# Routing rows of a mixture-of-experts kernel: first-choice rows leave once their indices exist, the row tags are rewritten in two parts, and GpSimd takes over two more output blocks and layer 1's early rows

## The reference, cut to what matters

```
x = L0_attn_x                                   # (32, 256, 128)
xn = layernorm(x)
x = x + attention_over_heads(xn) + experts0(xn) # layer 0
xn = layernorm(x)
x = x + long_convolution(xn) + experts1(xn)     # layer 1
return x

experts(x): logits = x @ W_gate                 # 8 experts
            top_w, top_i = top_k(logits, 2)     # weights by softmax
            out[t] = sum over the 2 choices of  w * (gelu(x[t] @ W_in[e] + b_in[e]) @ W_out[e] + b_out[e])
```

## Time and profile before

| what | value |
|---|---|
| runs, us | 1220.97, 1222.44, 1225.87 (median 1222.44) |
| profiled execution, span in us | 1227.7, with 19103 instructions |
| PE busy | 1013.8 us, 83% of the span |
| DVE busy | 747.2 us, 61% |
| POOL busy | 748.1 us, 61% |
| ACT busy | 584.5 us, 48% |
| chain that ended last, by engine | PE 37%, POOL 26%, DVE 14%, DMA 11%, issue 9%, ACT 3% |

### The profile page before, as it was taken

How to read it: one execution, slowest core, us unless ns; L and a number is a source line. 1 busy time by engine, 2 the same in 40 slices (tenths; PEclk the granted TensorE clock), 3 DMA queues, 4 the chain that set the end, 5 groups by cost and what they waited for, 6 DMA issues and landing times.

```text
span 1227.7 us, 19103 instructions
## 1 busy us (share of the span) xinstructions
PE 1013.8 (83%) x6498; PEld 856.5 (70%) x6498; DVE 747.2 (61%) x980; ACT 584.5 (48%) x1526; POOL 748.1 (61%) x655
## 2 busy tenths in 40 slices
PE   5646687789999999999435699999598999999994
PEld 4522333378888888888325699989588888888884
DVE  7877999999999999999989653111400200000018
ACT  1300110167777878778425872000066666666651
POOL 4147776558888888888674067677534544454430
PEclk9868887799999999999858699999899999999998
DMA  9913323326556565565271035999659676776749
GB/s 286 378 69 130 132 101 113 113 80 185 167 168 180 168 182 173 163 185 161 80 311 69 1 108 170 313 312 319 231 154 303 190 196 194 201 191 195 191 148 353
DMA packets 120245, 226.03 MB, mean 184 GB/s; under 512 B 16961, under 2 KB 80405, under 8 KB 118102
## 3 DMA queue, kind: packets, MB, share of 16 engines
q1 hardware_dynamic: 102164, 188.45, 50.5%
q0 software_dynamic: 17600, 35.71, 8.0%
q10 hardware_dynamic: 386, 0.66, 0.2%
HBM read 157.33 MB, written 67.42 MB: 183 GB/s over the span
## 4 chain that ended last, share of the span: by engine, by line
PE 37%; POOL 26%; DVE 14%; DMA 11%; issue 9%; ACT 3%; SPq 0%; POOLq 0%; DVEq 0%; ACTq 0%
POOL BG L319 12%; PE ps L819 9%; POOL y_tok L523 9%; PE ps L832 9%; PE ps L861 7%; DMA FF<-sorted_x 5%; POOL sorted_x L515 5%; DMA TPB<-in_kpad 3%; DVE BG L1168 3%; PE ps L927 2%; PE ps L806 2%; PE ps L774 1%; DVE stats L1023 1%; PE ps L937 1%; PE ps L963 1%
## 5 line engine op out<-in xcount | busy, mean ns | idle before, releaser
L523 POOL DMA_INDIRECT y_tok<-FF,yidx x284 | 277.8, 978 | 204.3 <-ACT FF L603 142.3
L515 POOL DMA_INDIRECT sorted_x<-XN,idx x256 | 246.5, 963 | 95.3 <-issue 85.6
L832 PEld LDWEIGHTS ps<-FF 128*128 128x128 f32 x2272 | 264.8, 192 | 19.6 <-issue 9.0
L832 PE MATMUL ps<-FF 128*128 128x128 f32 x2272 | 276.9, 275 | 0.0
L819 PE MATMUL ps<-FF 128*128 128x256 f32 x1136 | 272.1, 383 | 0.0
L593 ACT ACTIVATE FF<-ps,FF 128x256 f32<-128x256 f32 x568 | 231.8, 476 | 25.8 <-PE ps L819 25.0
L819 PEld LDWEIGHTS ps<-FF 128*128 128x128 f32 x1136 | 206.4, 192 | 23.3 <-ACT FF L593 0.6
L319 POOL TENSOR_TENSOR BG<-TPB 128x2048 f32<-128x2048 f32 (+1 forms) x42 | 166.5, 3991 | 13.2 <-DVE BG L1194 12.8
L1362 DVE TENSOR_TENSOR BG<-BG,ps 128x512 f32<-128x512 f32 x16 | 10.5, 685 | 230.9 <-PE ps L997 230.7
L861 PE MATMUL ps<-BG,cst 128*128 128x512 f32 x176 | 105.8, 769 | 50.8 <-DVE BG L1168 50.8
L1208 DVE TENSOR_TENSOR BG<-ps,TPB 128x1024 f32<-128x1024 f32 x128 | 147.5, 1216 | 0.0
(11 more groups left out here) (207 smaller groups left out, 1444.8 us busy)
## 6 DMA issues: line engine op xcount, KB each, us to landing
FF<-in_moe SPq DMA_DIRECT2D x142, 514.0 KB
TPB<-in_kpad SPq DMA_DIRECT2D x22, 1024.0 KB, 8.0
sorted_x<-TPB SPq DMA_DIRECT2D x36, 520.0 KB, 4.4
FF<-sorted_x SPq DMA_DIRECT2D x142, 130.0 KB, 2.2
BG<-y_tok SPq DMA_DIRECT2D x12, 1024.0 KB, 9.7
FF<-in_kpad SPq DMA_DIRECT2D x10, 1024.0 KB, 8.0
y_tok<-FF,yidx POOLq DMA_INDIRECT x284
xt_d<-BG SPq DMA_DIRECT2D x16, 256.0 KB, 3.9
```

What stands on the lines that cost most here:

```text
L515: pool.indirect_dma_start(sorted_x[layer], bass.IndirectOffsetOnAxis(ap=idx[:, k, j:j + 1], axis=0), XN[:, j, :], None).then_inc(s_sc, 16)
L523: pool.indirect_dma_start(y_d[layer], bass.IndirectOffsetOnAxis(ap=yidx[:, G % 4, r:r + 1], axis=0), ys[:, G % 4, r * D:(r + 1) * D], None ...
L832: t = pe.matmul(psY[:, r * P:(r + 1) * P], hT[:, G % 2, m, r * P:(r + 1) * P], wc[:, G % 4, HID + m * D:HID + (m + 1) * D], start=False, s ...
```

## The change

Six edits. First, `route_rows` adds to the semaphore `row_indices_ready` after each of the two index copies, not once after both; DVE's next products of the second choice no longer wait for the first copy. Second, `scatter` waits for one choice's indices at a time. Third, it rewrites tags and weights in two parts, tiles 0 to 47 and 48 to 63, with a semaphore for each, so that the rewrite of a part for k = 1 waits only for the DMAs of the same part of k = 0. Fourth, `ADD_POOL` becomes 6: blocks 4 and 5 move from DVE to GpSimd. Fifth, GpSimd makes all 16 rows of quarters 0 to 2 and ACT makes none. Sixth, the waits elsewhere are counted anew (`layer1_rows_ready` to 4; TensorE's wait before the convolution to 4).

```diff
-ROWS_POOL = 8
-ROWS_PARTS = 7
-
-ADD_POOL = 4
+ROWS_PARTS = 4
+TAGS_EARLY = 48
+
+ADD_POOL = 6
...
-        s_sc = sem("rows_scattered")
+        s_sc = [sem("early_rows_scattered"), sem("late_rows_scattered")]
...
-                sp.wait_ge(s_sc, 16 * 2 * NT * (layer + 1))
+                sp.wait_ge(s_sc[0], 16 * 2 * TAGS_EARLY * (layer + 1))
+                sp.wait_ge(s_sc[1], 16 * 2 * (NT - TAGS_EARLY) * (layer + 1))
...
             def scatter(layer):
-                pool.wait_ge(s_rows, layer + 1)
                 pool.wait_ge(s_zf[layer], 16 * NFILL)
                 if layer == 1:
                     pool.wait_ge(s_xnr, ROWS_PARTS)
                 for k in range(2):
-                    wait(pool, s_sc, 16 * NT * (2 * layer + k))
-                    pool.tensor_copy(XN[:, :, D + 1], wt[:, k, :])
-                    plink(pool.tensor_copy(XN[:, :, D].bitcast(u32), tags[:, k, :]))
-                    for j in range(NT):
-                        beside_tensor_engine(layer, k * NT + j)
-                        pool.indirect_dma_start(
-                            sorted_x[layer], bass.IndirectOffsetOnAxis(ap=idx[:, k, j:j + 1], axis=0),
-                            XN[:, j, :], None).then_inc(s_sc, 16)
+                    pool.wait_ge(s_rows, 2 * layer + k + 1)
+                    for part, (j0, j1) in enumerate(((0, TAGS_EARLY), (TAGS_EARLY, NT))):
+                        wait(pool, s_sc[part], 16 * (j1 - j0) * (2 * layer + k))
+                        pool.tensor_copy(XN[:, j0:j1, D + 1], wt[:, k, j0:j1])
+                        plink(pool.tensor_copy(XN[:, j0:j1, D].bitcast(u32), tags[:, k, j0:j1]))
+                        for j in range(j0, j1):
+                            beside_tensor_engine(layer, k * NT + j)
+                            pool.indirect_dma_start(
+                                sorted_x[layer], bass.IndirectOffsetOnAxis(ap=idx[:, k, j:j + 1], axis=0),
+                                XN[:, j, :], None).then_inc(s_sc[part], 16)
...
-                for j in range(16 * q, 16 * q + ROWS_POOL):
+                for j in range(16 * q, 16 * q + 16):
...
-            for q in range(3):
-                for j in range(16 * q + ROWS_POOL, 16 * q + 16):
-                    t = norm_rows(XN[:, j, 0:D], j, 0)
-                t.then_inc(s_xnr, 1)
...
-            pe.wait_ge(s_rows, 2)
+            pe.wait_ge(s_rows, 4)
...
-                    link(dve.tensor_copy(idx[:, k, :], ta))
-                dve.sem_inc(s_rows, 1)
+                    dve.tensor_copy(idx[:, k, :], ta).then_inc(s_rows, 1)
+                dve.wait_ge(s_rows, 2 * layer + 2)
```

## The result

| | before | changed |
|---|---|---|
| median, us (15 runs each) | 1222.44 | 1215.11 |
| lowest to highest | 1218.05 to 1229.52 | 1210.14 to 1220.01 |
| ratio, 95% interval | | 0.9929 [0.9912, 0.9946] |
| profiled execution, span in us | 1227.7 | 1208.4 |

By the medians the change makes the kernel 7.3 us faster, by the ratio 8.7; by the interval it is 6.6 to 10.8 us. The two profiled executions lie 19.3 us apart, because the one of before lies near the upper end of its kernel's spread and that of the change near the lower end. So the profiles have to be compared from a common mark. I take the start of GpSimd's first add of token outputs, which stands at 614.84 before and at 614.81 now.

A forecast was written before the change was run, and what follows sets the result against it. Bound: the chain of waits through the scatter into the expert stage. Terms 0.5 + 1.6 - 4.4 - 1.7 - 4.45 + 1.0 = -7.5 us took the median 1222.4 to 1214.9; 8 in 10 for 1207 to 1221.

The forecast's parts named there:

- (a): Layer 1's start, quarters on DVE: GpSimd's adds delay quarter 0, quarter 2 gains 5.3 back; gate logits +1.6 us.
- (b): Layer 1's start: without ACT's rows, DVE's idle time before copying TensorE's counts vanishes, -4.4 us.
- (c): Layer 1's start: the scatter's first choice leaves after its own indices, -1.7 us.
- wait at DMA 64: Middle of layer 1's scatter: the wait until all of the first choice has landed goes, -4.45 us.
- rewrites at DMAs 48 and 112: Layer 1's scatter: two rewrites added inside the choices at 0.5 us each, +1.0 us.
- gap at DMA 113: GpSimd's unexplained gap in the scatter, 6.23 us in layer 1, 5.57 in layer 0; taken as unchanged.
- last scatter DMA: End of layer 1's scatter: last DMA, issued at 885.71 before, forecast near 878; -8.0 us in the reflection's table.
- first rival: GpSimd's adds do not hold DVE up: quarters' term -5.3, sum -14.4, 1208.0 us; chance 0.14.
- The second: Rival: GpSimd's rows hold DVE as the adds do, 0.44 us per operation; sum -3.9, 1218.5 us; chance 0.19.
- third rival: GpSimd's scatter gap comes more often: sum +2.1, 1224.5 us, or 1230.7 with a third gap; chance 0.09.
- forecast's own range: Median 1212 to 1218 us, with (a) between +0.5 and +4 and the rewrites' bounds; chance 0.58.
- the +0.5: Layer 0's scatter: nothing won, the rewrite ahead of DMA 112 behind DMA 110's wait for DVE costs +0.5 us.

The follow-up runs named there:

- e1: Changed kernel with the adds of blocks 4 and 5 given back to DVE (ADD_POOL = 4); 1210.13 us, ratio 0.9908.
- e4: Changed kernel with GpSimd's adds of blocks 4 and 5 cut into four pieces each; 1212.89 us, ratio 0.9922.
- e3: Kernel before with the tag edits alone (early first choice, two-part rewrite), adds and rows as before; 1217.20 us, ratio 0.9953.
- e10: e1 with four DMAs more in layer 1's scatter (copies of DMAs 20 to 23 into a spare table); 1213.33 us, one run.
- e5: Kernel before, unedited, run and profiled a second time; 1224.91 us, one run.
- e8: e1 with four DMAs more in layer 0's scatter (copies of DMAs 61, 73, 85, 97 into a spare table); 1212.66 us, one run.
- e9: Changed kernel with block 5 given back to DVE, block 4 left on GpSimd; 1213.89 us, one run.
- e11: e7 with the weights of expert tiles 2 and 3 issued behind the first rows; 1209.37 us, ratio 0.9875.
- e12: e1 with one DMA more in layer 1's scatter (DMA 20 into a spare table); 1210.51 us, one run.
- e7: e1 with the tags parted at tile 49 in place of 48; 1210.42 us, ratio 0.9894.
- e2: Changed kernel with half the rows of quarters 0 to 2 given back to ACT; 1216.60 us, ratio 0.9949.
- e6: Changed kernel, unedited, run and profiled a second time; 1214.53 us, one run.

## Why the prediction was right, and where its sum was not

The time, 1215.11 against 1214.9, is nearer than the working deserves, and that is luck: the rows moved by 11.0 us where the sum has 8.0. By its own terms, in us, with the two pairs of profiles:

| term | forecast | first pair | second pair |
|---|---|---|---|
| (a) shift of quarter 3 | +1.6 | +1.6 | +1.1 |
| (b) from that shift to the counts | -4.4 | -5.3 | -5.4 |
| (c) counts to first DMA | -1.7 | -1.8 | -1.8 |
| wait at DMA 64 | -4.45 | -4.5 | -3.9 |
| rewrites at DMAs 48 and 112 | +1.0 | +0.6 | +0.6 |
| gap at DMA 113 | 0 | -1.7 | -1.2 |
| last scatter DMA | -8.0 | -11.0 | -11.0 |

(The terms leave some tenths over for single DMAs.)

(a) held in its parts: quarter 0's shift was out at 645.2 (forecast 644 to 646), quarter 2's statistics began at 656.1 (655 to 657). The first rival, harmless adds, is ruled out by the four waits and by e1. The second, rows that hold DVE as adds do, is out as well: beside the rows a step takes up to 0.28 in place of 0.18, and quarters 2 and 3 lose 0.6 together, against 1.0 in my sum. One reason was too narrow. I spoke of steps with two SBUF inputs, but L1035, which has one, waited 2.32 us, and gate rows waited in e4. The Trainium skill, page "SBUF — State Buffer", section "Who interferes with whom", names `tensor_scalar` among the operations that can take the shared pair; the trace agrees for the adds, while DVE's steps beside GpSimd's rows do not show the whole-instruction lock that it states (0.1 us of 0.45). Between rows and DVE's adds it is GpSimd that waits: beside the four adds of blocks 6 and 7 the rows of quarter 2 took 11.02 us in all, where those of quarter 0 took 7.25.

(b) had the right mechanism, as e3 against e10 shows: 4.8 us, of which 0.4 are a shorter wait for quarter 3's gate rows (5.03 in place of 5.42). In the changed kernel the same wait makes the 0.9 above the forecast: TensorE came sooner through these gate rows, for which DVE waited 5.41 us before

```profile
684.69 0.56 DVE L1081 TENSOR_TENSOR TPB<-ps,best 128x384 f32<-128x384 f32 x1 [5.41 <-PE ps L774]
```

and 4.49 now:

```profile
685.30 0.56 DVE L1079 TENSOR_TENSOR TPB<-ps,best 128x384 f32<-128x384 f32 x1 [4.49 <-PE ps L772]
```

A window of before (busy time of each engine, then the granted clock, where 0.50 is 1.2 GHz and 1.00 is 2.4 GHz) shows a slower TensorE there

```profile
680.00:682.00 2.00, 2.00 (x16) 2.00 (x14) 0.00 (x0) 0.47 (x1) 0.00 (x0) 0.72 0.00 0
```

than one of the changed kernel, where quarter 3's shift stands one and a half microseconds later:

```profile
681.00:683.00 2.00, 2.00 (x20) 2.00 (x20) 0.00 (x0) 0.66 (x2) 0.00 (x0) 1.00 0.03 8
```

The fourteen profiles bear it out that this wait goes with the clock. Where TensorE's clock comes back from 1.2 GHz only 7.3 to 7.6 us behind quarter 3's shift, the wait is 5.29 to 5.42 (before, e3, e4, e5); at 6.8 it is 5.03 (e10), at 5.4 to 6.1 it is 4.37 to 4.66 (the changed kernel's first, e8, e9, e11, e12), and where it is back within 4.8, or is not down at all, 4.31 to 4.32 (e1 and e7; e2 and e6). What moves the slow stretch is open. It is not that DVE's adds of blocks 4 and 5 are gone from between the gate rows of quarters 1 and 2: in e1 they are there,

```profile
683.01 0.56 DVE L1079 TENSOR_TENSOR TPB<-ps,best 128x384 f32<-128x384 f32 x1 [4.31 <-PE ps L772]
```

and in e4 they are not:

```profile
684.84 0.56 DVE L1084 TENSOR_TENSOR TPB<-ps,best 128x384 f32<-128x384 f32 x1 [5.29 <-PE ps L777]
```

The mis-sized step is "The gap ahead of DMA 113 I leave as it is": it fell by 1.2 to 1.7 us in layer 1, and by 1.2 to 1.6 in layer 0. Where it stands at DMA 113 in kernels with the tags parted at 48, it is 3.9 to 5.4; in both profiles of before 5.5 to 6.2. That the tag edits shorten it is shown by e3; how they do it is as open as the gap itself. With the clock's 0.9 and the rewrites' 0.4 that makes the 3 us between forecast and rows. The third rival, more gaps, did not occur. The upper end of the forecast's own range is a slip: its bounds, +4 for (a) and 1.5 for the rewrites, add up to 1218.8 and not 1218.

Layer 0 gave nothing, though the +0.5 has the wrong sign: DMA 110 waits for DVE as forecast (220.97 against 221.36), but the gap behind it shrank too, and the last scatter DMA comes 1.4 us earlier. The last output DMA of its expert stage stands at 607.6 against 607.7, and the first add at the same time: that stage swallowed it in this pair. In the second pair the first add is 1.7 us earlier (615.49 against 617.17), but the two profiles of the kernel before differ by more, 2.3 us, so a small gain in layer 0 could not be seen. And the chain does not run through layer 0's scatter in every execution, as I took it to do: in e5, and in both profiles of the changed kernel, it passes it by, through TensorE's matmuls for the attention heads (L861, L859 in the changed kernel) and DVE's products. There a scatter that ends earlier has nothing to win.

So the scatter won 11.0 us, not 8.0, and the first tile 10.2 to 10.8 (the last rows took 2.38 and 3.06 us to land), while the medians moved by 7.3 and the ratio says 8.7. The interval, 6.6 to 10.8, just holds what the profiles show. The two single runs of e5 and e6 lie 10.4 apart. Whether some 2 us are given back somewhere, or the runs happened to lie close, stays open; no stage of the two pairs shows it.

## What to carry to other kernels

Before an engine's work is moved to another one to balance them, look at whose instructions it will run beside: here two blocks moved from DVE to GpSimd freed 5.3 us and cost 0.6 to 3.7 us more than that (shift 3 in e6 against e10, and in the changed kernel against e1), because a chain of 0.2 us steps met adds of 2.35 us. A wait for a small result (the counts) can be made by an engine that seems off the path (ACT's rows, which held the evacuation that TensorE needed). When a chain of DMAs is shortened, see what the DMA engines are doing at its end: issuing 2.9 us earlier won nothing for the first tile until other transfers were moved behind it, as far as one profile of each kernel tells.

## What was not expected of the hardware

- Steps of 0.06 us either way decide 2.2 us: a DVE product that begins just ahead of GpSimd's add takes 0.42 us, one that begins just behind it 2.54.
- GpSimd stops once in each scatter, at DMA 113, for 3.9 to 6.2 us. Four more DMAs in a scatter take the stop away; a rewrite of 0.6 us just ahead of the 114th DMA leaves 0.5 to 1.0 us of it. For what it stops was not found.
- The same kernel's layer 1 expert stage took 287.1 and 281.0 us in two executions, 5.1 of the difference in TensorE's waits for loads of sorted rows (14.2 against 9.1).
- The same gate rows kept DVE waiting 4.31 to 5.42 us, by how long TensorE's granted clock stood at 0.50 in them.
